# The last loop of batch norm: residual rows on GpSimd, a third of the adds with them, statistics three tiles behind

## The reference, cut to what matters

```python
h = layernorm(x)
g = attention(h, edges) + bias                      # 6250 x 256
g = (g - mean(g, 0)) * rsqrt(var(g, 0) + eps) * gamma + beta
x1 = x + (g + h)                                    # GNN branch adds h again, the outer residual adds x
l = layernorm(x1)
out = x1 + moe(layernorm(l), softmax(l @ Wr + br))  # top 2 of 8 experts, gelu between W1 and W2
```

## Time and profile before

| | |
|---|---|
| time, median of 3 runs | 1916.98 us (1916.75 to 1917.1) |
| profiled execution | the page gives its span, 1914.8 us; its own time is not given apart from it |
| PE, VectorE, ScalarE, GpSimd busy | 88%, 73%, 58%, 64% |
| x1 loop on VectorE | 1228.2 to 1268.7 us |
| routing until the experts' first gather | 1268.7 to 1312.6 us |
| experts | from 1312.6 us to the end |

### The profile page before, as it was taken

One profiled execution on the slowest core, in us unless ns is written; L12 is line 12 of the kernel. 1 busy time (PEld: TensorE's weight loads), 2 busy tenths in 40 slices (PEclk: granted clock), 3 DMA queues, 4 the chain that ended last, 5 costly groups with the idle time before them and its releaser, 6 DMA issues.

```text
span 1914.8 us, 37627 instructions
## 1 busy us (share of the span) xinstructions
PE 1680.9 (88%) x10798; PEld 1177.1 (61%) x10798; DVE 1394.5 (73%) x3802; ACT 1106.1 (58%) x2385; POOL 1216.6 (64%) x1157
## 2 busy tenths in 40 slices
PE   6679898998988989889898888845999999999997
PEld 5445554554545545445454544633989889888896
DVE  6686877877778777787777878897666666666664
ACT  3555676767667666676666765773343443434443
POOL 1377777777777777777777777202556666566653
PEclk9889899999999999998999999977999999999999
DMA  8655446455564555645555444592233323323222
GB/s 282 212 147 145 123 141 166 121 154 158 142 167 119 155 158 142 167 121 154 156 145 163 125 130 113 191 346 103 46 49 50 53 46 55 49 47 54 48 44 35
DMA packets 124146, 240.41 MB, mean 126 GB/s; under 512 B 25064, under 2 KB 82996, under 8 KB 122772
## 3 DMA queue, kind: packets, MB, share of 16 engines
q0 software_dynamic: 62800, 147.76, 32.8%
q1 hardware_dynamic: 51816, 80.51, 12.8%
q10 hardware_dynamic: 9340, 9.73, 1.5%
HBM read 195.47 MB, written 43.30 MB: 125 GB/s over the span
## 4 chain that ended last, share of the span: by engine, by line
PE 44%; POOL 25%; DVE 11%; issue 10%; DMA 7%; ACT 1%; DVEq 1%; POOLq 0%; ACTq 0%; SPq 0%
POOL gather_ring L1115 24%; PE bank L2067 15%; PE bank L2084 14%; PE bank L1240 7%; DMA gather_ring<-node_table,src_slot 4%; PE bank L1206 4%; DVE acc L1139 2%; PE bank L720 1%; PE bank L2048 1%; DVE gather_ring L1167 1%; DVE piece_max L1074 1%; DVE feat L1408 1%; DMA raw_idx<-src_pad,edge_tile_i 1%; ACT r_ring L1392 1%; PE bank L975 1%
## 5 line engine op out<-in xcount | busy, mean ns | idle before, releaser
L1115 POOL DMA_INDIRECT gather_ring<-node_table,src_slot x879 | 838.2, 954 | 268.1 <-issue 254.7
L1206 PE MATMUL bank<-ones 128*128 128x512 bf16 x1787 | 562.0, 395 | 75.4 <-ACT gather_ring L1281 64.1
L1240 PE MATMUL bank<-gather_ring,onehot 128*128 128x264 f32 x1758 | 569.1, 407 | 49.6 <-DVE gather_ring L1167 49.0
L1240 PEld LDWEIGHTS bank<-gather_ring,onehot 128*128 128x128 f32 x1758 | 298.7, 196 | 258.6 <-DVE gather_ring L1167 214.2
L1139 DVE TENSOR_TENSOR acc<-acc,bank 128x264 f32 x879 | 370.4, 421 | 22.7 <-PE bank L1240 21.2
L1167 DVE TENSOR_TENSOR gather_ring<-gather_ring,bank 128x256 f32<-128x256 f32 x879 | 362.1, 412 | 0.3 <-ACT bank L1280 0.3
L2152 POOL DMA_INDIRECT out_rows<-y,token_idx x105 | 201.8, 1922 | 219.6 <-DMA out_rows<-y,token_idx 155.3
L1206 PEld LDWEIGHTS bank<-ones 128*128 128x128 bf16 x1787 | 171.9, 100 | 223.2 <-issue 102.8
L2121 ACT ACTIVATE hid<-bank,cols 128x256 f32<-128x256 f32 (+1 forms) x448 | 209.8, 550 | 141.6 <-PE bank L2067 138.6
L2067 PE MATMUL bank<-xe,w_hi 128*128 128x256 f16 (+1 forms) x1792 | 284.3, 267 | 0.6 <-ACT hid L2121 0.5
L2084 PE MATMUL bank<-w,hid_hi 128*128 x1680 | 278.3, 273 | 0.0
(11 more groups left out here) (315 smaller groups left out, 1963.2 us busy)
## 6 DMA issues: line engine op xcount, KB each, us to landing
w_stage<-in_L_ffn_W SPq DMA_DIRECT2D x16, 1024.0 KB, 7.9
dst_row<-dst_rows SPq DMA_DIRECT2D x110, 128.0 KB, 3.5
gather_ring<-node_table,src_slot POOLq DMA_INDIRECT x879
w_split<-w_out SPq DMA_DIRECT2D x32, 256.0 KB
w<-w_split SPq DMA_DIRECT2D x8, 1024.0 KB, 9.4
node_table<-acc ACTq DMA_DIRECT2D x24, 264.0 KB
r_ring<-in_x_lanes SPq DMA_DIRECT2D x7, 896.0 KB, 6.7
xt<-in_x_lanes SPq DMA_DIRECT2D x24, 256.0 KB, 4.7
```

Source lines behind the costliest of these rows:

```text
L1115: e.indirect_dma_start(out=gather_ring[:, b % GB, j, :], out_offset=None, in_=node_table, in_offset=bass.IndirectOffsetOnAxis(ap=src_slot[ ...
L1206: e.matmul(to[:, :].rearrange("p (k n) -> p k n", k=2), halves[:, 0:P], halves.rearrange("p (a n) -> p a n", a=1).broadcast_to([P, 2, 2 * ...
L1240: e.matmul(bank[AGG[s % len(AGG)]][:, 0:ROW], onehot[:, b % OHB, j, :], gather_ring[:, b % GB, j, :], start=True, stop=True).then_inc(summ ...
```

## The change

All 49 residual rows move from ScalarE to GpSimd, in a new function `pool_x1` that runs after `pool_iotas` and ahead of `pool_ffn`. Tiles with n % 3 == 1 (16 of them) are "joined": ScalarE copies their 256 result columns from PSUM to acc, and GpSimd adds the residual row to them there; the other 33 are added by VectorE as before. GpSimd's queue holds residual n and then join n - 16. VectorE's stats(n) stands three tiles behind, and `variances(0)` two iterations later. The semaphores are counted apart for the two kinds of tile, and SP's wait for a group asks for both.

```diff
-        RESID_AHEAD, LATE_AT = 24, 16
+        RESID_AHEAD, STATS_BEHIND, JOIN = 16, 3, 3
+        def joins(n):
+            return n % JOIN == 1
+        def joined_up_to(n):
+            return (n + JOIN - 2) // JOIN
         def wait_x1(e, g):
-            e.wait_ge(x1_made, (g + 1) * NG)
+            n = (g + 1) * NG
+            e.wait_ge(x1_made, n - joined_up_to(n))
+            e.wait_ge(x1_joined, joined_up_to(n))
...
# scalar_norm: gone
-            for n in range(RESID_AHEAD):
-                scalar_resid(e, n)
...
+        def pool_x1(e):
+            def resid(n):
+                g = n // NG
+                if n % NG == 0:
+                    wait_x_again(e, g)
+                rows = r_ring[:, g % RB, n % NG, :]
+                e.tensor_scalar(rows, rows, rstd[:, n:n + 1], x_shift[:, n:n + 1], ALU.mult, ALU.add).then_inc(resid_made, 1)
+            def join(n):
+                e.wait_ge(scaled_kept, joined_up_to(n + 1))
+                e.wait_ge(resid_made, n + 1)
+                e.tensor_tensor(acc[:, n, 0:D], acc[:, n, 0:D], r_ring[:, n // NG % RB, n % NG, :], ALU.add
+                                ).then_inc(x1_joined, 1)
+            for n in range(NT + RESID_AHEAD):
+                if n < NT:
+                    resid(n)
+                if n >= RESID_AHEAD and joins(n - RESID_AHEAD):
+                    join(n - RESID_AHEAD)
...
# vector_x1
             def stats(n):
-                e.wait_ge(x1_made, n + 1)
+                if joins(n):
+                    e.wait_ge(x1_joined, joined_up_to(n + 1))
+                else:
+                    e.wait_ge(x1_made, n + 1 - joined_up_to(n + 1))
...
-            for n in range(NT + 1):
-                if n < NT:
+            for n in range(NT + STATS_BEHIND):
+                if n < NT and not joins(n):
                     x1(n)
-                if n:
-                    stats(n - 1)
-                if n == 4 * NG:
+                if n >= STATS_BEHIND:
+                    stats(n - STATS_BEHIND)
+                if n == 4 * NG + STATS_BEHIND - 1:
                     variances(0)
...
# scalar_stage3, keep_logits
-                    e.wait_ge(x1_made, n + 1)
+                    if joins(n):
+                        e.wait_ge(x1_scaled, n + 1)
+                        e.activation(by_half(acc[:, n, 0:D]), scaled_rows(n), ACT.Copy).then_inc(scaled_kept, 1)
+                    else:
+                        e.wait_ge(x1_made, n + 1 - joined_up_to(n + 1))
                     e.activation(logits[:, n, :], x1_bank(n)[:, P:P + NE], ACT.Copy).then_inc(logits_kept, 1)
-                    if n + RESID_AHEAD < RB * NG:
-                        scalar_resid(e, n + RESID_AHEAD)
-                    elif LATE_AT <= n < LATE_AT + NT - RB * NG:
-                        scalar_resid(e, n - LATE_AT + RB * NG)
...
             pool_iotas(e)
+            pool_x1(e)
             pool_ffn(e)
```

More of the change, by code:

```diff
@@ L1314, in build_gnn_moe @@
         x_again = [sem(f"x_again{i}") for i in range(RB)]
-        resid_made = sem("resid_made")
+        resid_made, scaled_kept, x1_joined = sem("resid_made"), sem("scaled_kept"), sem("x1_joined")
         X_AGAIN = 16
@@ L1386, in stage3_loads @@
             e.dma_start(br_row[:, :], br.rearrange("(a n) -> a n", a=1).broadcast_to([P, NE])).then_inc(stage3_rows, 16)
[L1388 to L1393, removed]
         def tiles_in(c):
@@ L1533, in by_half, with scaled_rows @@
             return ap.rearrange("p (k m) -> p k m", m=P)
+        def scaled_rows(n):
+            return x1_bank(n)[:, 0:KD * (P + NE)].rearrange("p (k m) -> p k m", m=P + NE)[:, :, 0:P]
+        def pool_x1(e):
[15 more added lines that the diff above has]
+                    join(n - RESID_AHEAD)
         def vector_x1(e):
@@ L1539, in x1 @@
                 e.wait_ge(x1_scaled, n + 1)
-                both = x1_bank(n)[:, 0:KD * (P + NE)].rearrange("p (k m) -> p k m", m=P + NE)[:, :, 0:P]
-                e.tensor_tensor(by_half(acc[:, n, 0:D]), both, by_half(r_ring[:, g % RB, n % NG, :]), ALU.add
+                e.tensor_tensor(by_half(acc[:, n, 0:D]), scaled_rows(n), by_half(r_ring[:, g % RB, n % NG, :]), ALU.add
                                 ).then_inc(x1_made, 1)
             def stats(n):
-                e.wait_ge(x1_made, n + 1)
+                if joins(n):
+                    e.wait_ge(x1_joined, joined_up_to(n + 1))
+                else:
+                    e.wait_ge(x1_made, n + 1 - joined_up_to(n + 1))
                 vector_order.of(e.bn_stats(bn6[:, n, :], acc[:, n, 0:D]))
@@ L1847, in rows @@
                 made.then_inc(rows_made, 1)
-            assert GROUPS == RB + 2 and RESID_AHEAD + LATE_AT > RB * NG
+            assert GROUPS == RB + 2
             for g in range(5):
```

## The result

Timed side by side (21 runs of each), the changed kernel takes 1921.16 us against 1917.75, a ratio of 1.0018 (95% interval 1.0012 to 1.0024): 2.3 to 4.6 us slower. A later timing on another occasion gave 1.0006 (0.9997 to 1.0015). I had forecast 1910.3 us, 6.7 less than before. The profiled execution of the changed kernel has a span of 1915.2 us and a time of its own of 1917.4, the shortest of the 21.

A forecast was written before the change was run, and what follows sets the result against it. VectorE's rate was taken to bound the x1 loop, with a ScalarE stall at its head. Gain 10.1 - 1.4 - 1.5 - 0.5 = 6.7 us, giving 1910.3 us; range 1905.8 to 1915.0.

The forecast's parts named there:

- What bounds the kernel: x1 loop: VectorE's rate limits it, ScalarE stalls its head; each microsecond saved starts the expert stage one sooner.
- The stall and the clock behind it: Head of the x1 loop: VectorE's 3.57 us stall and about 2.2 us of lower PE clock would go.
- my sign of being right: Profile after: PE's clock at 1.00 throughout, among other signs such as last stats at 1261 to 1263 us.
- VectorE's floor: x1 loop: 33 x1 and 49 stats at 0.33 us plus 2.36 of small chains; 10.1 us gain if GpSimd is never late.
- GpSimd's durations: x1 loop: 0.46 us a residual row, 0.58 an add; GpSimd's lateness takes 1.4 us out of the gain.
- 31 R + 11 J: GpSimd's time from first join through residual 48: 31 residuals of R and 11 joins of J, 20.6 us.
- The clash before the loop: VectorE's chain ahead of the first matmul: operations waiting for GpSimd's residuals cost 0 to 4 us, 1.5 taken.
- The clash within the loop: Ten small VectorE operations inside the x1 loop wait for GpSimd: 0 to 2 us, 0.5 taken.
- Rival B: x1 loop: GpSimd is slow enough to eat the gain, 1917 us at 0.68 us a residual; chance 0.13.
- my signs of being wrong: Stats waiting for GpSimd every third tile, a residual over 0.6 us, chain operations over twice their length, or GpSimd awaiting loads.
- The experts "unchanged and merely earlier": Routing and expert stage after the loop: the same length as before, only starting sooner.
- Rivals D and E: D: group 6's load up to 3.1 us late, 1913.4; E: pre-loop clash at its upper bound, 1913.8; together 0.13.

The follow-up runs named there:

- e2: Kernel before, with ScalarE making 12 instead of 24 residual rows ahead of the first logits, late ones from tile 24 instead of 16; ratio 0.9973.
- e7: Kernel before, plus 18 unused tensor_scalar of 128x256 on GpSimd beside VectorE's chain ahead of the loop; single run 1917.5 us.
- e8: Kernel before, plus 32 unused memsets of 128x256 on GpSimd beside VectorE's chain ahead of the loop; single run 1914.8 us.
- e3: Changed kernel with all residual rows back on ScalarE, 12 ahead, so that GpSimd only adds every third tile; ratio 0.9929.
- e11: Kernel before, unedited, profiled a second time; 603.6 us from the experts' first gather to the end of the span, no ratio given.
- e12: Changed kernel with every sixth tile joined instead of every third; ratio 1.0014 (0.9982 to 1.0045).
- e4: Changed kernel without joined tiles: GpSimd makes all 49 residual rows, VectorE adds all tiles; ratio 1.0017 (0.9988 to 1.0046).

## Why the prediction was wrong

*What bounds the kernel.* Right. The loop's end goes straight to the experts' first gather: the routing between took 44.3 us before and after.

*The stall and the clock behind it.* Right: 3.57 + 2.2 = 5.8 us forecast, 5.5 measured in e2's c. In the changed kernel PE's clock is 1.00 from 1232 to 1264 us. It was not 1.00 throughout, as my sign of being right had it: it fell ahead of the loop.

*VectorE's floor.* Right in its instructions (starts 0.33 us apart; 33 and 49 of them), too low by the clashes inside.

*GpSimd's durations: the step that failed, with the clash before the loop.* I took 0.46 us for a residual and 0.58 for an add. They start 0.53 and 0.71 us after one another. The sum 31 R + 11 J, my 20.6 us, measures 1257.18 - 1232.66 = 24.5: 3.9 us. The copies of 128 and 8 columns gave the slope of a copy and not of a two-operation tensor_scalar; for the add I scaled a 1792-column row through nearly zero, with a fixed part of 0.12 us for which I had no row. 3210 ns and 732 ns together give an estimate of (3210 - 732)/1536 = 1.61 ns a column and a fixed part of 0.32 us. A small slip stands beside it: 1249.8 + 9.2 + 1.34 is 1260.3 and not 1260.0.

*The clash before the loop.* 1.5 us assumed, 1231.67 - 1228.21 = 3.5 measured (a: 3.6 to 3.8, once 4.7). Of a's 3.6, 2.8 are the waits I had described: eleven operations, 0.26 us each in the mean. That is the lower end of the 3 to 4 us that I had worked out, and I halved it without a row, although I had one for the full price: L414 waited out GpSimd's iota in the earlier trace rows. The other 0.8 is a term that I had put at nothing: PE, kept waiting by the stretched chain, comes back at the lower clock. That the range up to 4 us held the sum of both is luck. Here the Trainium skill (SBUF — State Buffer, Summary: rules for kernel authors) was the better guide. By its rule a VectorE operation with two inputs in SBUF is blocked by a GpSimd operation that reads; e7 and e8 agree (0.30 to 0.50 us beside reads, 0.16 beside writes). One in a two-port mode is blocked by any; e8's tensor_scalars were held up by memsets, though no row shows their mode. It also says that the blocked one waits until the first finishes; e8, 3.65 us through a train of memsets, does not agree.

*The clash within the loop.* 0.5 us assumed. variances(0) went from 1.02 to 2.05 - 0.33 = 1.7 us and gains(0) from 0.67 to 1.56 - 0.33 = 1.2; the second counted whole. The first fell partly where GpSimd held the pace: unstretched, stats(31) would have waited for the add that ends at 1256.50; it started at 1256.87, so 0.3 to 0.4 us of it counted too.

Together they account for the miss. Forecast end of the loop 1262.0; + 2.0 (before the loop: 1.3 of waits and 0.8 of clock over the 1.5 assumed, less 0.2 by which batch norm began sooner) + 3.9 (GpSimd) + 0.1 (clash within, gains(0) alone) = 1268.0; measured 1266.67 + 1.39, the last four stats: 1268.06. What is left out on one side (the part of variances(0) that counted) and the slip of 0.3 us on the other are of that size too, so the agreement to 0.1 us is partly luck. Before it was 1268.69, so of 10.1 us to be had 0.6 stayed. In these two profiles d is 1.0 us longer, and 0.6 lies outside the span, which is more than that gain. Rival B described it: the mechanism was in the text, at 0.13. Of my signs of being wrong two came true (stats waiting 0.56 us at every third tile for a stretch, operations of the chain at three times their length); a residual over 0.6 us did not.

*The experts "unchanged and merely earlier".* Not clearly so. d is 602.2 to 603.6 us before and 602.8 to 603.8 after. The moment at which PE's granted clock goes from 0.50 to 1.00 in the experts' first slot differs from profile to profile and may have a part in it. In the first profile of the kernel before the mean clock of ten microseconds there is 0.86, in e3's 0.74 (stretches: length, busy of the engines, clock, DMA share, GB/s; d is 604.2 in e3):

```profile
1322.60:1332.60 10.00, 9.51 (x75) 7.91 (x74) 4.04 (x12) 6.12 (x11) 2.12 (x3) 0.86 0.17 49
```

```profile
1566.30:1576.30 10.00, 9.50 (x64) 7.36 (x63) 2.96 (x11) 5.01 (x9) 2.21 (x3) 0.74 0.18 51
```

But that moment alone does not set d: e11 has a clock of 0.87 there and a d of 603.6, e12 has 0.81 and the longest d, 605.8. So a microsecond or more comes or goes with no change in the experts' code, in the kernel before as well, and its cause stays open. Rivals D and E: no wait of GpSimd for a load stands in the changed kernel's waits; E priced the clash at 3.5 us over the forecast, and about 2.1 of that came, a third of the 6.1 us by which the loop ended late.

## What to carry to other kernels

Work given to an idle engine is priced twice: by its own rate over all that stands in that queue within the span of the loop (three rows and an add, 2.30 us, against 1.65 on VectorE), and by what it does to VectorE's small operations while it runs, above all to a chain of dependent ones ahead of the loop: 2.8 us here, and 0.8 more because PE, kept waiting, came back at its lower clock. Look first for the one stall that can be had by itself: here a number in ScalarE's head, 5.5 us of the loop, where moving all rows to GpSimd for its sake gained nothing clear (e4: 1.3 us of the loop at most). Split the moved work by what each engine has left, and start it behind the chain: 7.5 us of the loop, 6.3 to 6.7 of the time.

## What the runs showed of the hardware that I had not expected

- A VectorE tensor_scalar of 264 columns beside back-to-back GpSimd memsets did not get in between them: 3.65 us for two, until the last memset, while two-column operations with two inputs kept 0.16 us.
- PE's granted clock was 0.50 for a time after it had waited 3.0 to 4.0 us for the chain (changed kernel, e7, e8), and stayed at 1.00 where it had waited 0.97 (before). It cost 0.8 to 1.9 us until the first x1.
- GpSimd's tensor_scalar with two operations and two per-row columns over 256 columns: 566 ns in the mean, starts 0.53 us apart; its tensor_tensor of 256 columns: 732 ns, 0.71 apart.
- A GpSimd residual is hardly slowed by VectorE's x1, stats and two-column operations (0.55 to 0.57 us each). Beside VectorE's tensor_scalars of 264 columns one took 0.69 us in the changed kernel and two took 0.70 in e7.
